# First attention stage: head outputs turned to rows by TensorE products, and a pitch of 68 words for keys and values

## What is computed

```
B, L, D, H = x.shape[0], x.shape[1], 512, 32        # the linear layers carry a bias
q, k, v = (x @ W.T + b).reshape(...)                # float32 throughout
scores  = einsum over the 16 numbers of a head, among the 32 heads of one row
att     = softmax(scores)
out     = att @ v                                   # per row: 32 heads x 16 numbers
x       = layernorm(x + out)
```

## Time and profile before

| | us (or as said) |
|---|---|
| median of three runs | 2864.88 |
| lowest, highest | 2859.4, 2866.1 |
| profiled execution, its own time | 2859.8 |
| span of its profile | 2858.5 |
| mean granted TensorE clock | 0.976 |
| PE busy, whole span | 2684.5 (94%) |

### The profile page before, as it was taken

One profiled execution on the slowest core, in us unless ns is written; L12 is line 12 of the kernel. 1 busy time (PEld: TensorE's weight loads), 2 busy tenths in 40 slices (PEclk: granted clock), 3 DMA queues, 4 the chain that ended last, 5 costly groups with the idle time before them and its releaser, 6 DMA issues.

```text
span 2858.5 us, 37899 instructions
## 1 busy us (share of the span) xinstructions
PE 2684.5 (94%) x14840; PEld 1634.0 (57%) x14840; DVE 1580.6 (55%) x2793; ACT 774.2 (27%) x2502; POOL 382.8 (13%) x455
## 2 busy tenths in 40 slices
PE   8959999999999789899999999998998888999998
PEld 7735555555555566555555555556774455566664
DVE  3535555555556577555655555555666653344455
ACT  0101222222233233212222222322333512333331
POOL 1012111111111100121111111122120031000002
PEclk9979999999999899999999999999999999999999
DMA  7840101101000100001011010010000020000000
GB/s 167 141 140 23 37 23 37 38 15 37 15 15 37 67 2 1 27 23 37 23 37 36 17 37 8 22 67 30 2 2 27 1 80 27 14 16 10 12 1 30
DMA packets 87409, 98.92 MB, mean 35 GB/s; under 512 B 62496, under 2 KB 71648, under 8 KB 81088
## 3 DMA queue, kind: packets, MB, share of 16 engines
q1 hardware_dynamic: 87232, 96.49, 11.7%
HBM read 85.99 MB, written 10.49 MB: 34 GB/s over the span
## 4 chain that ended last, share of the span: by engine, by line
PE 87%; DVE 6%; DMA 2%; issue 1%; ACT 1%; SPq 1%; POOL 1%; DVEq 0%; POOLq 0%; ACTq 0%
PE banks L589 19%; PE banks L628 16%; PE banks L608 4%; PE banks L638 4%; PE banks L581 4%; PE banks L1578 3%; PE banks L1068 3%; PE banks L1630 3%; PE banks L320 2%; PE banks L1900 2%; PE banks L1868 2%; PE banks L1933 2%; PE banks L1607 2%; PE banks L1583 2%; PE banks L618 2%; PE banks L1646 2%
## 5 line engine op out<-in xcount | busy, mean ns | idle before, releaser
L628 PE MATMUL banks<-weights,OT 128*128 128x512 f32 x1024 | 464.7, 597 | 5.9 <-DMA weights<-in_L_xwo 5.4
L589 PE MATMUL banks<-xT,weights 128*128 128x512 f32 x1024 | 457.9, 592 | 0.0
L664 ACT ACTIVATE E_x<-S_x,sm_x 128x128 f32<-128x128 f32 x512 | 199.2, 390 | 545.9 <-DVE sm_x L717 545.9
L589 PEld LDWEIGHTS banks<-xT,weights 128*128 128x128 f32 x1024 | 189.1, 190 | 210.4 <-issue 210.4
L697 DVE TENSOR_TENSOR turned<-banks,const 64x512 f32<-64x512 f32 x160 | 109.5, 684 | 356.0 <-PE banks L589 355.8
L628 PEld LDWEIGHTS banks<-weights,OT 128*128 128x128 f32 x1024 | 185.8, 191 | 192.6 <-issue 185.6
L746 POOL TENSOR_TENSOR QT<-QT,turned 128x512 f32<-128x512 f32 x128 | 162.2, 1267 | 785.3 <-DVE QT L699 785.3
L1989 ACT ACTIVATE E_s<-banks,top_s 128x128 f32<-128x128 f32 x512 | 139.3, 383 | 288.1 <-DVE top_s L2086 288.1
L161 POOL TENSOR_TENSOR norm_spread<-norm_mv,const 128x1 f32<-128x1 f32 x96 | 20.9, 218 | 1243.4 <-DVE norm_mv L157 1243.4
L726 DVE TENSOR_TENSOR E_x<-E_x,sm_x 128x512 f32<-128x512 f32 x128 | 179.4, 1402 | 4.4
L678 ACT ACTIVATE OT<-banks 128x512 f32<-128x512 f32 x128 | 76.5, 597 | 387.3 <-PE banks L638 387.3
(11 more groups left out here) (279 smaller groups left out, 4094.7 us busy)
## 6 DMA issues: line engine op xcount, KB each, us to landing
weights<-in_L_xwq SPq DMA_DIRECT2D x16, 1024.0 KB, 4.9
weights<-in_L_xwo SPq DMA_DIRECT2D x16, 1024.0 KB, 4.9
weights<-in_L_xwk SPq DMA_DIRECT2D x16, 256.0 KB, 5.3
weights<-in_L_xwv SPq DMA_DIRECT2D x16, 256.0 KB, 5.4
weights<-in_L_ffn_W_base SPq DMA_DIRECT2D x3, 1024.0 KB, 5.0
weights<-in_L_xwq SPq DMA_DIRECT2D x4, 768.0 KB, 4.9
weights<-in_L_xwo SPq DMA_DIRECT2D x4, 768.0 KB, 5.8
xT<-in_xT SPq DMA_DIRECT2D x4, 512.0 KB, 9.5
```

The source lines that it names most:

```text
L589: mm = PE.matmul(bank[:, :], weight, source[:, k, half_of(i)], start=k == 0, stop=k == KC - 1)
L628: mm = PE.matmul(psum[7][:, :], OT[u % 2][:, h, :], wo[:, h, :], start=h == 0, stop=h == 3)
L664: ins = AC.activation(e[:, j, :], s[:, j, :], ACT.Exp, bias=sm[:, 0, j:j + 1], scale=1.0, accum_out=sm[:, 1, j:j + 1])
```

## The change

- `turn_back(q)` on PE replaces the way through DRAM. For each of the 16 numbers d of a head it makes two products with a 64 column choice of the unit matrix: stationary `o16[:, :, :, d]` (64 columns at a step of 16 words), moving the 64 unit columns `(a, c, h)` of one c (two runs of 32), output on partitions 64 c to 64 c + 63. That is 32 matmuls per quarter, into banks 0 and 1, for q = 3 into banks 4 and 5. It waits for `h_o(4q+4)` and signals `h_back`.
- `add(q)` reads these two banks directly (`turned_back`): output element (h, d) lies at h + 64 d words. `O`, `scratch["o"]`, and the DMAs of L270 and L277 are gone.
- Order: PE makes turn_back(q) after jobs(q+2, 1 to 2) and before jobs(q+2, 3); turn_back(2) after values(2); turn_back(3) after values(3). scores(1) and scores(2) wait for the add of the quarter before in place of its outputs. DVE makes add(0) and add(1) between drains (q+2, 2) and (q+2, 3), and add(2) with normalise(4, 5) before outputs(3). The load of x[:, 0:4] moves from q = 1 to q = 0. `load_next` follows directly on `late_rows`.
- K and V get a pitch of 68 words: `[P, 4, 32, 68]` and `[P, 4, 17, 68]`; loads fill 64 words of each 68. q16 keeps its 64.

```diff
-                K = sbuf("k_blocks", [P, 4, HEADS, 64], scope)
-                V = sbuf("v_blocks", [P, 4, V1, 64], scope)
+                K = sbuf("k_blocks", [P, 4, HEADS, PITCH], scope)
+                V = sbuf("v_blocks", [P, 4, V1, PITCH], scope)
...
+                def turned_back(q, half):
+                    at = 4 if q == 3 else 0
+                    return banks[:, at:at + 2, :].rearrange("p n (d a h) -> p a h (n d)", a=2, h=HEADS)[:, half, :, :]
...
-                        if q:
+                        if q == 0:
                             SP.dma_start(x[:, 0:4, :], dram["x"][:, 0:4, :]).then_inc(*rows_in.one())
                         store(q + 1, range(4, 6))
                         store(q + 2, range(1))
                         load_v(q + 1)
-                        store_outputs(q)
-                        store(q + 2, range(1, 3))
-                        outputs_back(q)
-                        store(q + 2, range(3, 4))
+                        store(q + 2, range(1, 4))
...
-                    store_outputs(2)
-                    outputs_back(2)
                     following = load_next()
-                    store_outputs(3)
-                    outputs_back(3)
...
                             if 0 < q < 3:
-                                PE.wait_ge(*h_o(4 * (q - 1) + n + 1))
+                                PE.wait_ge(*h_sum(2 * q))
...
+                    def turn_back(q):
+                        PE.wait_ge(*const_in.all())
+                        PE.wait_ge(*h_o(4 * q + 4))
+                        for d in range(HD):
+                            to = psum[(4 if q == 3 else 0) + d // 8]
+                            for c in range(2):
+                                picked = ident.rearrange("p (a c h) -> p a c h", a=2, c=2)[:, :, c, :]
+                                mm = PE.matmul(to[64 * c:64 * c + 64, d % 8 * 64:(d % 8 + 1) * 64], o16[:, :, :, d].rearrange("p j i -> p (j i)"), picked, start=True, stop=True)
+                        mm.then_inc(*h_back.one())
...
                         values(q)
                         if q + 2 < QUARTERS:
-                            jobs(q + 2, range(1, 4))
+                            jobs(q + 2, range(1, 3))
+                        turn_back(q)
+                        if q + 2 < QUARTERS:
+                            jobs(q + 2, range(3, 4))
...
                         outputs(q)
-                        if q:
-                            add(q - 1)
                         if q + 2 < QUARTERS:
-                            drains(q + 2, range(1, 4))
+                            drains(q + 2, range(1, 3))
+                            add(q)
+                            drains(q + 2, range(3, 4))
                     normalise(range(4))
                     centre(3)
                     turn(3)
+                    add(2)
+                    normalise((4, 5))
                     outputs(3)
-                    for q in range(2, 4):
-                        add(q)
-                        normalise((2 * q, 2 * q + 1))
+                    add(3)
+                    normalise((6, 7))
```

More of the change, by code:

```diff
@@ L191, in build @@
         HEADS, HD, QUARTERS, QT_ = 32, 16, 4, T // 4
-        V1 = HD + 1
-        scratch = {n: nc.dram_tensor(f"scratch_{n}", (T * D,), F32, kind="Internal").ap() for n in "qkvo"}
+        V1, PITCH = HD + 1, 68
+        scratch = {n: nc.dram_tensor(f"scratch_{n}", (T * D,), F32, kind="Internal").ap() for n in "qkv"}
         h_w_in = [signal(f"heads_w{n}_in", 16) for n in "qkv"]
@@ L198, in build @@
         h_qk_in, h_v_in = signal("heads_qk_in", 16), signal("heads_v_in", 16)
-        h_o_stored, h_o_in = signal("heads_o_stored", 16), signal("heads_o_in", 16)
         h_score, h_centred, h_exp, h_pt = (signal(f"heads_{n}") for n in ("scored", "centred", "exped", "pt_here"))
-        h_mix, h_o, h_sum = (signal(f"heads_{n}") for n in ("mixed", "o_here", "x_added"))
+        h_mix, h_o, h_back, h_sum = (signal(f"heads_{n}") for n in ("mixed", "o_here", "o_turned", "x_added"))
         late_rows_in = signal("late_rows_in", 16)
@@ L230, in between_heads @@
                 o16 = sbuf("o16", [P, 4, 16, HD], scope)
-                O = sbuf("O_s0", [P, 2, D], scope)
                 small = [sbuf(f"sm{n}_s0", [P, 2, 16], scope) for n in range(4)]
@@ L236, in between_heads @@
                 v_view = scratch["v"].rearrange("(h d q j a) -> q j h d a", h=HEADS, d=HD, q=4, j=4)
-                o_view = scratch["o"].rearrange("(q p f) -> q p f", q=4, p=P)
-                o_back = scratch["o"].rearrange("(q r h t d) -> q r t h d", q=4, r=4, h=HEADS, d=HD)
                 def in32(n):
                     return slice(32 * n, 32 * n + 32)
+                def turned_back(q, half):
+                    at = 4 if q == 3 else 0
+                    return banks[:, at:at + 2, :].rearrange("p n (d a h) -> p a h (n d)", a=2, h=HEADS)[:, half, :, :]
                 def bank_of(q, n):
@@ L258, in load_qk @@
                             SP.dma_start(q16[32 * r:32 * r + HD, :, :], qk_view["q"][q, r]).then_inc(*h_qk_in.one())
-                            SP.dma_start(K[32 * r:32 * r + HD, r, :, :], qk_view["k"][q, r]).then_inc(*h_qk_in.one())
+                            SP.dma_start(K[32 * r:32 * r + HD, r, :, 0:64], qk_view["k"][q, r]).then_inc(*h_qk_in.one())
                     def load_v(q):
@@ L265, in load_v @@
                         for j in range(4):
[L266 to L273, removed]
-                        if q:
-                            SP.wait_ge(*h_sum(2 * q))
-                        for r in range(4):
-                            SP.dma_start(O[64 * (r % 2):64 * (r % 2) + 64, r // 2, :].rearrange("p (h d) -> p h d", d=HD), o_back[q, r]).then_inc(*h_o_in.one())
+                            SP.dma_start(V[in32(j), j, 0:HD, 0:64], v_view[q, j]).then_inc(*h_v_in.one())
                     store(0, range(4))
@@ L353, in pe_heads @@
                         if q + 2 < QUARTERS:
-                            jobs(q + 2, range(1, 4))
+                            jobs(q + 2, range(1, 3))
+                        turn_back(q)
+                        if q + 2 < QUARTERS:
+                            jobs(q + 2, range(3, 4))
                     scores(3)
-                    PE.wait_ge(*const_in.all())
                     for b in range(4):
@@ L359, in pe_heads @@
                     values(3)
+                    turn_back(3)
                     for b in range(4, 7):
@@ L413, in outputs @@
                             if q and n == 0:
-                                DV.wait_ge(*h_o_stored(q))
+                                DV.wait_ge(*h_back(q))
                             DV.tensor_tensor(o16[:, :, 4 * n:4 * n + 4, :], found[:, :, :, 0:HD], inverse_sums, ALU.mult).then_inc(*h_o.one())
@@ L418, in add @@
                         DV.wait_ge(*(rows_in if q < 2 else late_rows_in).all())
-                        DV.wait_ge(*h_o_in(4 * q + 4))
+                        DV.wait_ge(*h_back(q + 1))
                         if q == 2:
@@ L423, in add @@
                             b = 2 * q + half
-                            DV.tensor_tensor(x[:, b, :], O[:, half, :], x[:, b, :] if q < 2 else v["late_rows"][:, b - 4, :], ALU.add).then_inc(*h_sum.one())
+                            rows = x[:, b, :] if q < 2 else v["late_rows"][:, b - 4, :]
+                            DV.tensor_tensor(x[:, b, :].rearrange("p (h d) -> p h d", d=HD), turned_back(q, half),
+                                             rows.rearrange("p (h d) -> p h d", d=HD), ALU.add).then_inc(*h_sum.one())
                     def normalise(bs):
```

## The result

The changed kernel takes 2847.22 us in the median (2846.35 to 2848.21), the kernel before 2865.49 in the same measurement: a ratio of 0.994, 95% interval 0.9923 to 0.9957. That is faster by 0.6%, inside the forecast range of 2826 to 2852 and 6 us above the 2841 that was named. The medians are 18.3 us apart, and the interval reaches from 12 to 22 us of gain; the forecast gain was 21. The spans of the two profiled executions differ by 2858.5 - 2845.9 = 12.6 us; the profiled execution before, at 2859.8 us, is among the shortest of its kernel, hence the smaller difference.

The account below looks back on a forecast made before the run. It took PE, busy 94% of the span, as the bound, the first stage judged by itself: second stage at 163.8 for 184.9, 21.1 us less, 2838.7 profiled or 2843.8 against the median; it took 2841, range 2826 to 2852.

Parts of the forecast that it names:

- The tail, removed: End of first stage: 30.8 us from last division to add fall away, less turn_back(3)'s products and the last division's delay.
- The unit products: turn_back on PE: 32 products a quarter at 81 ns each, 2.6 us a quarter, bounds 1.7 and 3.8.
- the prediction's own rule: Each further microsecond per quarter of unit products costs about 3.8 us.
- The pitch, taken at nothing: K and V at 68 words: no effect on PE's reads assumed; bound 3.9 us a quarter gained on scores, or slower DMA writes.
- the loads of K and V get slower: Rival: each load takes 4 us more at the new pitch, 8 us lost, gain 13, 2849 us; chance 0.12.
- The pitch pays: Rival: step of 17 lines spreads PE's reads, scores fall to 29 ns, gain 33, 2829 us; chance 0.30 for 3 us or more.
- The x load: Load of 1 MB of x ahead of quarter 0's v stores: 3.3 to 3.7 us delay moves from quarter 1 to 0.
- The keys of quarter 3: Before scores(3): keys come at 136.6, before PE is ready; the products fill the 5.09 us wait.
- Quarter 3: Last quarter: turning to 149.4, add(2) and normalise(4, 5) 4.6 us on the path, divisions to 156.6, products to 159.2.
- Next stage's weights: load_next at 143.6 instead of 151.64; context lands at 152.3, first product's needs are met by 156: hidden.
- The add on stepped banks: DVE's add reading PSUM at a step of 64 words: 1.29 us for two, at most double, 1.3 us on the path once.
- The unit products run one after the other: Rival: column halves don't overlap, 415 ns a product, 13.3 us a quarter, 2884 us, slower than before; chance 0.04.

Follow-up runs that it names:

- a_add_late: The changed kernel at a pitch of 64 words, with add(2) and normalise(4, 5) after outputs(3) instead of before it: 2842.22 us, ratio 0.9927 to the kernel before.

## Why the prediction was right, and where its terms were off

The tail was understood, and it is the gain. The number was met only within a range 26 us wide: two terms were off the same way, 9.8 us together by places, and against the prediction's own sum for the profiled execution (2838.7) the 2847.3 is 8.6 us long. By two of the signs that it named it was wrong in part: the first product of the second stage came at 172.7 us, outside 160 to 169, and turn_back waited over 1 us in quarter 0. A third sign came true: keys landed in over 8 us, the cost of the pitch.

Places from the start of scores(0), forecast, changed kernel, and the same at a pitch of 64:

| | forecast | measured | at 64 |
|---|---|---|---|
| scores(1) | 36.1 | 40.5 | 36.5 |
| scores(2) | 71.3 | 77.4 | 73.1 |
| scores(3) | 93.3 | 101.1 | 96.6 |
| second stage | 119.2 | 129.0 | 123.6 |

- *The tail, removed*: right in place and size. What follows the last division (164.11) is the products, 0.5 us until the add, and 4.1 us of adding, scaling and turning (168.59 to 172.72) for a forecast 4.6; the turned block took 0.66 us for 1.12.
- *The unit products*: mis-sized, 3.85 us a quarter for 2.6, at the upper bound of 3.8. Two faults met. I took a price per instruction from the rows and multiplied by the 32 products of the source, where the trace has 64 instructions. And the step of the stationary side is not a part of the price but half of it: 60 ns an instruction for 32 with adjacent columns. That the bounds of 1.7 and 3.8 us lie so near the two forms (2.0 and 3.85) is luck: the upper one was 32 times 118 ns, where the trace has 64 times 60, half the count at twice the price. The 59 ns of a stepped score instruction, not doubled for its 64 columns and counted 64 times, would have given the number too, though no run shows which side paces that row. By the prediction's own rule this is 3.8 x 1.25 = 4.8 us on the path. The column "at 64" shows 4.4: after quarter 0 each part is later by 1.1 to 1.5 us, and in quarter 0 by 0.4 only, since the forecast wait of 0.9 us did not come.
- *The pitch, taken at nothing*: it cost 5.4 us. The named rival "the loads of K and V get slower" came about beside the forecast: 1.5 to 2 us a load and not 4, and in the main (4.0 us) in quarter 0, where its mechanism (PE waits for the divisions) was told. 4.4 + 5.4 = 9.8 are the way from the forecast +119.2 to +129.0.
- *"The pitch pays"*: shown wrong for 68 and 80. The rule of the Trainium skill, SBUF — State Buffer, section "Door 1: The DMA port swizzle" (each access on another 16 byte line pays) named no gain from the pitch, and the runs agree in that; that 68 and 80 words are slower than 64 it does not say.
- *The x load*: moved from quarter 1 to 0, its delay changed place as forecast, in size only about: at a pitch of 64 the drain of quarter 0 comes 2.4 us later after its scores than before, and that of quarter 1 4.0 us earlier, for 3.3 to 3.7. So PE had none of the 0.9 us wait there; at 68 it had 3.2.
- *The keys of quarter 3*: right. The 5.09 us wait is filled by the products and no wait for keys is left.
- *Quarter 3*: right. From the end of the scores to the end of turning it is 3.9 us, then 4.5 us of add(2) and normalise for a forecast 4.6, then 2.6 us of divisions. What it does not see is that values(3) lie beside these steps, so putting them behind the divisions brings the divisions 2.3 us forward (a_add_late) and not 4.6.
- *Next stage's weights*: hidden as forecast. The context landed at 148.8 + 12.0 = 160.8 for a forecast 152.3, 12 us ahead of the first product, as the forecast had it (163.8 - 152.3 = 11.5).
- *The add on stepped banks*: 1.29 us for two, exactly as before; the doubling did not come.
- *"The unit products run one after the other"*: did not come; 60 ns each against 288 of their own length.

## What to carry to other kernels

Before a way through DRAM is replaced by work on a busy engine, look at what its time consists of: here 16.8 of 30.8 us were a place in a queue behind 6 MB, and one line of order brought most of the gain. Put the replacing work only where the engine is idle; without the products on its packed part the kernel was 10 us faster (2833.66 for 2844.00), 8 of them before the last scores. Price a product per instruction as the trace counts it, and lay out the stationary operand of small products with adjacent words. The rows speak for the same on the moving side, but no run changed it.

## What the runs showed of the hardware

- A stepped stationary operand halves the rate of the 64 column products, 60 for 32 ns, and that pace does not change with the granted clock (3.85 us at 0.58 and at 1.00), while the adjacent form goes from 2.0 us at 1.00 to 3.4 at 0.55. For the moving side no run changed the step alone: the 59 ns for 29 come from two stages, and the stationary side is stepped in one of them. The values, whose stationary side is adjacent, have the same price per stepped moving column (30.5 ns for 68).
- DVE reads two PSUM banks at a step of 64 words without loss (1.29 us for two operations), but writes SBUF at a step of 64 words slower (0.60 us for 0.42).
- A destination pitch of 272 bytes for pieces of 256 bytes lengthens the median landing of the key loads to 8.2 to 9.2 us in four kernels, from 6.9 to 7.5 in eight with a pitch of 256 bytes. At 320 bytes it is 7.6 us in one kernel, hardly longer, though most pieces there lie off multiples of 256 bytes of the tile as well.
- Two microseconds of gain ahead of a dense stretch can be lost in it: the first 16 instructions of the second stage took 7.03 us at a granted 1.00, 8.73 at 0.80, 9.6 at 0.73. Unread products in the waits before them brought 7.03 back. The same low clock on the stepped unit products costs nothing.
